# Value products a step later, query products first, the next input transposed in the gate bank, and TensorE's loop from step 80

## The reference

```python
x = x + tanh(g_xattn[0]) * L0_xattn(layernorm(x), ctx, mask)   # 32 query heads, 8 kv heads of 128
x = x + tanh(g_ffn[0])   * L0_ffn(layernorm(x))                # MX fp6 x fp4 weights, silu(gate) * up, then down
x = x + tanh(g_xattn[1]) * L1_xattn(layernorm(x), ctx)
x = x + tanh(g_ffn[1])   * L1_ffn(layernorm(x))                # columns permuted, int4 weights

# L1_xattn: q = h @ Wq.T, k = ctx @ Wk.T, v = ctx @ Wv.T, by heads
q, k = rmsnorm(q, q_norm_w), rmsnorm(k, k_norm_w)              # per head
probs = softmax(q @ k.T / sqrt(128) + mask)
out = (probs @ v) @ Wo.T
```

## Time and profile before

| what | value |
|---|---|
| median of three runs | 1319.82 us |
| profiled execution, its span | 1320.3 us, 1318.5 us |
| TensorE matmul busy | 1302.9 us, 99% of the span |
| VectorE (DVE) busy | 1001.4 us, 76% |
| ScalarE (ACT) busy | 867.4 us, 66% |
| GpSimd (POOL) busy | 621.9 us, 47% |
| chain that ended last: TensorE, GpSimd, VectorE, DMA | 76%, 6%, 5%, 3% |

### The profile page before, as it was taken

How to read it: one execution, slowest core, us unless ns; L and a number is a source line. 1 busy time by engine, 2 the same in 40 slices (tenths; PEclk the granted TensorE clock), 3 DMA queues, 4 the chain that set the end, 5 groups by cost and what they waited for, 6 DMA issues and landing times.

```text
span 1318.5 us, 25473 instructions
## 1 busy us (share of the span) xinstructions
PE 1302.9 (99%) x7477; PEld 1102.0 (84%) x7493; DVE 1001.4 (76%) x2106; ACT 867.4 (66%) x3356; POOL 621.9 (47%) x683
## 2 busy tenths in 40 slices
PE   8999999999999999999999999999999999999999
PEld 7888888888888888877777788888888888888887
DVE  6878787887878788688888858777767677677656
ACT  5767667676767776645566456777767767676551
POOL 2546566565656666446677533532323323332232
DMA  7011110211121121020301013532232222321101
GB/s 297 1 57 55 63 55 20 68 48 68 50 68 50 35 71 33 13 64 20 103 20 48 20 48 89 161 64 77 60 67 69 40 70 57 80 56 32 17 8 56
DMA packets 87340, 78.34 MB, mean 59 GB/s; under 512 B 70880, under 2 KB 75872, under 8 KB 83168
## 3 DMA queue, kind: packets, MB, share of 16 engines
q1 hardware_dynamic: 70272, 71.91, 18.6%
q10 hardware_dynamic: 16672, 4.46, 1.6%
q0 software_dynamic: 320, 1.05, 0.2%
HBM read 57.48 MB, written 3.15 MB: 46 GB/s over the span
## 4 chain that ended last, share of the span: by engine, by line
PE 76%; issue 8%; POOL 6%; DVE 5%; DMA 3%; ACT 1%; POOLq 0%; ACTq 0%; DVEq 0%; SPq 0%
PE bank L1298 54%; PE bank L1362 6%; PE bank L1290 6%; PE bank L1393 6%; PE bank L1324 2%; DMA p_turned<-p_planes 2%; POOL w_lo L551 2%; POOL rstd L580 2%; PE bank L1479 1%; PE bank L1379 1%; POOL fw_y L591 1%; POOL fw_y L589 1%; DVE probs L1138 1%; ACT squares L769 1%; DMA ctx_raw<-in_ctxT 0%
## 5 line engine op out<-in xcount | busy, mean ns | idle before, releaser
L551 POOL TENSOR_TENSOR w_lo<-w_raw,w_hi (+1 forms) x150 | 192.8, 1303 | 164.7 <-ACT w_hi L730 164.7
L769 ACT ACTIVATE squares<-bank 128x128 bf16<-128x128 f32 x512 | 134.4, 278 | 184.7 <-PE bank L1298 184.5
L711 ACT ACTIVATE probs<-probs,negmax 128x128 f32<-128x128 f32 x512 | 198.2, 391 | 7.1 <-DVE negmax L1010 4.5
L576 POOL TENSOR_TENSOR meansq<-sumsq,scalars 128x5 f32<-128x5 f32 x128 | 27.5, 215 | 354.1 <-ACT squares L769 354.1
L580 POOL TENSOR_TENSOR rstd<-meansq,scalars 128x5 f32<-128x5 f32 x128 | 153.2, 1197 | 10.7 <-POOL meansq L576 1.1
L1298 PE MATMUL bank<-w_hi,oT_hi 128*128 (+1 forms) x512 | 150.9, 416 | 0.0
L1298 PE MATMUL bank<-w_hi,xT_hi 128*128 (+1 forms) x512 | 140.3, 395 | 0.0
L1298 PE MATMUL bank<-w_lo,xT_hi 128*128 (+1 forms) x512 | 138.1, 390 | 0.3
L1362 PEld LDWEIGHTS bank<-kT,qT 128*128 128x128 f32 x1024 | 131.7, 191 | 7.7
L1298 PE MATMUL bank<-w_hi,oT_lo 128*128 (+1 forms) x512 | 138.0, 391 | 0.0
L1298 PE MATMUL bank<-w_lo,oT_hi 128*128 (+1 forms) x512 | 137.6, 390 | 0.0
(11 more groups left out here) (129 smaller groups left out, 3073.1 us busy)
## 6 DMA issues: line engine op xcount, KB each, us to landing
w_raw<-in_wq SPq DMA_DIRECT2D x16, 1024.0 KB, 4.8
w_raw<-in_wo SPq DMA_DIRECT2D x16, 1024.0 KB, 9.8
w_raw<-in_wkv SPq DMA_DIRECT2D x16, 512.0 KB, 5.6
fw_raw<-in_ffn_w SPq DMA_DIRECT2D x36, 192.0 KB, 2.3
x_sb<-in_x SPq DMA_DIRECT2D x7, 256.0 KB, 10.7
ctx_raw<-in_ctxT SPq DMA_DIRECT2D x7, 256.0 KB, 9.7
fw_raw<-in_ffn_w SPq DMA_DIRECT2D x7, 256.0 KB, 2.7
out<-x_sb SPq DMA_DIRECT2D x7, 256.0 KB, 2.0
```

The lines of the kernel that those rows point to most:

```text
L551: last = nc.gpsimd.tensor_tensor(lo, raw, hi.bitcast(FP32), ALU.subtract)
L576: nc.gpsimd.tensor_tensor(meansq[:, :], sumsq[:, :], eps_sb[:, :], ALU.add).then_inc(ms_done, 1)
L711: last = nc.scalar.activation(probs[:, h * P:(h + 1) * P], probs[:, h * P:(h + 1) * P], ACT.Exp, bias=negmax[:, h:h + 1], accum_out=rowsum ...
L769: last = nc.scalar.activation(squares[:, h // 2, (b + 1) % 4, h % 2, :], q_bank(n, kind)[:, h * P:(h + 1) * P], ACT.Square, scale=SCALE, a ...
```

## The change

Four edits, of which the last is small:

- **Value products late.** In the PLAIN steps and the steps 76 to 124 (`values_late`) TensorE does the query products first, then the first third of the key/value products, then the value products of unit n-3 (before: of unit n-2, at the end of the step), the rest of the key/value products, scores, output, transposes of k and q. On ACT the squares of q come first, then `oT_hi`, the square of k, `v_hi`; `p_whole` and `pT_hi` go to the end of the step, behind `qT`. On DVE `pT_lo` goes ahead of the planes, and `p_whole` to the end of the step; the int4 work and `wp_lo` (one step later) move ahead of `oT_lo`.
- **Next input in the gate products' bank.** The transposes of the next layer's input use psA instead of psC. They wait for the hidden values of the feed-forward (`gated`) instead of for the accumulation of its output (`d_acc`), and the down products no longer wait for their reader; the gate products do.
- **TensorE's loop from step 80.** Its program has the PLAIN loop from step 80 on (five iterations in place of four); the other engines' loops stay at 88.
- One weight piece moves from step 81 to 82, one from 82 to 83; the normalising of the first batch for the int4 product moves ahead on DVE.

```diff
@@ pieces of the weights
-              32: ((E + 1, 6), (E + 1, 7)), 33: ((E + 1, 8), (E + 1, 9), (E + 2, 0)), 34: ((E + 2, 1), (E + 2, 2)),
-              35: ((E + 2, 3),), 36: ((E + 2, 4), (E + 2, 5)), 37: ((E + 2, 6),), 38: ((E + 2, 7), (E + 2, 8)),
+              32: ((E + 1, 6), (E + 1, 7)), 33: ((E + 1, 8), (E + 1, 9)), 34: ((E + 2, 0), (E + 2, 1)),
+              35: ((E + 2, 2), (E + 2, 3)), 36: ((E + 2, 4), (E + 2, 5)), 37: ((E + 2, 6),), 38: ((E + 2, 7), (E + 2, 8)),
@@ steps
-        def run_steps(eng, step, drain=None):
+        def run_steps(eng, step, drain=None, plain=ZONE1):
...
-            for s in range(ZONE0, ZONE1):
+            for s in range(ZONE0, plain):
...
+        def values_late(n, kind):
+
+            return kind == PLAIN or (isinstance(n, int) and DMA0 < n <= DMA1)
...
         def xT_bank(m):
-            return psC
+            return psA if BATCHES <= m < 2 * BATCHES else psC
@@ ACT
+                    if values_late(n, kind):
+                        q_squares(n, b, kind)
+                        output_upper(n)
                     act.wait_ge(kv_ps, n + 1)
...
                     act.wait_ge(qk_ps, n + 1)
                     nc.scalar.activation(qT[:, :], psSQ[:, :], ACT.Copy).then_inc(qT_sb, 1)
+                if has(n, 2) and by_dma(n, kind):
+
+                    act.wait_ge(pv_ps, n - 2)
+                    act.wait_ge(planes_turned, (n - DMA0 + 1) * 16)
+                    nc.scalar.activation(halves(p_whole[:, :])[:, :, 1], p_turned[:, 0:KT, :].rearrange("p k t -> p (k t)"),
+                                         ACT.Copy).then_inc(upper_placed, 1)
+                    act.wait_ge(upper_placed, n - DMA0 + 2)
+                    act.wait_ge(lower_placed, n - DMA0 + 2)
+                    nc.scalar.activation(pT_hi[:, :], p_whole[:, :], ACT.Copy).then_inc(pt_hid, 1)
@@ DVE
+            def whole_lower(n):
+
+                dve.wait_ge(pt_hid, n - 2)
+                nc.vector.tensor_tensor(pT_lo[:, :], p_whole[:, :], pT_hi[:, :].bitcast(FP32),
+                                        ALU.subtract).then_inc(pt_lod, 1)
+
+            def output_lower(n):
+
+                dve.wait_ge(o_hid, n - 2)
+                nc.vector.tensor_tensor(oT_lo[:, :], psPO[:, :], oT_hi[:, :].bitcast(FP32),
+                                        ALU.subtract).then_inc(o_lod, 1)
...
+                if by_dma(n, kind) or t.last == 0:
+                    scaled_probs(n)
+                if values_late(n, kind):
+                    whole_lower(n)
                 if by_dma(n, kind):
-                    scaled_probs(n)
                     probs_planes(n)
+                for k in gathered(n - 1, kind):
...
+                if kind == ZONE and 0 <= n - INT4_0 < INT4_PARTS and values_late(n, kind):
+                    int4_weights(n - INT4_0)
+                if values_late(n, kind):
+                    output_lower(n)
@@ TensorE
+                        if c == 0 and i >= 2:
+                            pe.wait_ge(xT_lod, BATCHES + i - 1)
...
+                def values(lag=2):
+                    pe.wait_ge(pt_lod, n + 1 - lag)
+                    if lag == 3:
+                        pe.wait_ge(o_lod, n - 3)
+                    slot = (b - lag) % 4
...
+                    if values_late(n, kind):
+                        queries()
+                        wait(pe, kT_sb, n)
+                        keys_values(slice(0, KT))
+                        values(3)
+                        keys_values(slice(KT, 3 * KT)).then_inc(kv_ps, 1)
...
-                    pe.wait_ge(d_acc, t.next + 1)
-                    transposes(qn, psC, ident[:, :]).then_inc(xT_ps, 1)
+                    pe.wait_ge(gated, len(CHUNKS) * min(t.next + 2, BATCHES))
+                    transposes(qn, psA, ident[:, :]).then_inc(xT_ps, 1)
...
-                    if t.next is not None:
-                        pe.wait_ge(xT_lod, BATCHES + t.next + 1)
```

More of the change, by code:

```diff
@@ L730, in split_upper, with q_squares, output_upper @@
                     nc.scalar.activation(hi, raw, ACT.Copy).then_inc(split_hi, 1)
+            def q_squares(n, b, kind):
+                act.wait_ge(q_ps, n + 1)
+                wait(act, rs_done, n)
+                if values_late(n, kind):
+                    act.wait_ge(qk_ps, n)
+                for h in range(REP):
+                    dump = (qn[:, h * P // 2:(h + 1) * P // 2].bitcast(BF16) if values_late(n, kind)
+                            else squares[:, h // 2, (b + 1) % 4, h % 2, :])
+                    last = nc.scalar.activation(dump, q_bank(n, kind)[:, h * P:(h + 1) * P], ACT.Square, scale=SCALE,
+                                                accum_out=sumsq[:, h:h + 1])
+                return last
+            def output_upper(n):
+                act.wait_ge(pv_ps, n - 2)
+                wait(act, y_ps, n - 3)
+                nc.scalar.activation(oT_hi[:, :], psPO[:, :], ACT.Copy).then_inc(o_hid, 1)
             def step(n, b, kind, j, q=None):
@@ L734, in step @@
                 exp_late = calm(n, kind) or (kind == FIRST and b == BATCHES - 1)
[L735 to L739, removed]
+                if has(n, 3) and not values_late(n, kind):
+                    output_upper(n)
                 if calm(n, kind) or (kind == ZONE and n == FFN0):
@@ L764, in step @@
                     hidden_turned(0, t.down)
[L765 to L771, removed]
+                if has(n, 0) and not values_late(n, kind):
+                    q_squares(n, b, kind).then_inc(sq_done, 1)
                 if t.first is not None:
@@ L781, in step @@
                     gate_tanh(2, t.down)
[L782 to L790, removed]
                 if has(n, 2) and not by_dma(n, kind):
@@ L1028, in place_lower, with last_normalised, probs_lower @@
                                       ).then_inc(lower_placed, 1)
-            def probs_lower(n, kind=None):
+            def last_normalised(i):
+                wait(dve, xT_ps, 2 * BATCHES + i if i else 0)
+                normalise(NORM["last", i], i, f_s[:, :])
+            def whole_lower(n):
[6 more added lines that the diff above has]
+                                        ALU.subtract).then_inc(o_lod, 1)
+            def probs_lower(n):
                 dve.wait_ge(pt_hid, n - 1)
-                nc.vector.tensor_tensor(pT_lo[:, :], (p_whole if by_dma(n, kind) else psPO)[:, :], pT_hi[:, :].bitcast(FP32),
+                nc.vector.tensor_tensor(pT_lo[:, :], psPO[:, :], pT_hi[:, :].bitcast(FP32),
                                         ALU.subtract).then_inc(pt_lod, 1)
@@ L1096, in step @@
                     row_inverse(n)
-                if has(n, 2) and not t.active and not by_dma(n, kind):
+                if has(n, 2) and not t.active and not by_dma(n, kind) and t.last != 0:
                     scaled_probs(n)
@@ L1105, in step @@
                         ctx_lower(t.first)
-                if kind == ZONE and 0 <= n - INT4_0 < INT4_PARTS:
+                if kind == ZONE and 0 <= n - INT4_0 < INT4_PARTS and not values_late(n, kind):
                     int4_weights(n - INT4_0)
[L1108 to L1112, removed]
                 if t.first is not None:
@@ L1115, in step @@
                     normalise(t.first, t.first, f_s[:, :])
-                if t.last is not None:
-                    wait(dve, xT_ps, 2 * BATCHES + t.last if t.last else 0)
-                    normalise(NORM["last", t.last], t.last, f_s[:, :])
+                if t.last is not None and t.last:
+                    last_normalised(t.last)
                 if t.norm is not None:
@@ L1149, in step @@
                 if has(n, 2) and qn_first(n, kind, t) and not calm(n, kind):
[L1150 removed]
+                    probs_lower(n)
                 if t.next is not None:
@@ L1524, in _ @@
             first_q(0, slice(2 * KT, 3 * KT)).then_inc(q_ps, 1)
-            run_steps(pe, step)
+            run_steps(pe, step, plain=ZONE1 - BATCHES)
 _SHAPES_OUT = [((BATCHES, P, D), "float32")]
```

69 lines of the change are left out of this document (37 added, 32 removed).

## The result

The changed kernel took 1340.35 us (median of four runs, 1338.17 to 1342.37) against 1319.99 before: a ratio of 1.0156, 95% interval 1.0142 to 1.017. The forecast was no difference, 1320.8, with a range to 1327. It was wrong, by some 20 us. The profiled execution has a span of 1340.6 us.

A forecast was written before the change was run, and what follows sets the result against it. TensorE is busy nearly throughout, so its products plus waits bound the kernel. 1320.3 - 7.7 + 1.9 + 6.75 + 0.06 = 1321.3, less 0.5 to the median: 1320.8 us; no difference 1317.2 to 1322.5, range 1311.5 to 1327.

The forecast's parts named there:

- the branch: TensorE's loop: one added branch costs 0.06 us, so the skill's rule on taken branches breaking instruction fetch moves nothing.
- What goes: TensorE, steps 75 to 124: stalls from late k-transpose landings (7.25) and the f_s wait (0.46) vanish, 7.7 us gained.
- PLAIN's two-piece steps: DVE, 12 PLAIN steps: first plane 0.08 ahead of POOL, one w_lo passes, oT_lo ends at Q+5.5, hidden.
- Steps 77, 78 and 84 to 87: DVE: work ahead of oT_lo meets w_lo; stalls 1.5, 2.0, 1.35 each in 84 and 86, 0.28 each in 85 and 87; 6.75 us.
- Steps 79 to 83: ZONE: 0.03 us between planes and POOL's w_lo left undecided; half the 0.75 stall taken, 1.9 us, bounds 0 and 3.75.
- The floor: TensorE's undisturbed step stays at 9.06 us, since the products are the same; 1.5 us either way over 49 steps.
- The bank: Next input's transposes waiting for the hidden values: 0.29 us to spare in a feed-forward step, so 0.
- The loop from 80: TensorE's loop starting at step 80 adds one branch, 0.06 us.
- POOL gets in first in the PLAIN loop too: Rival, DVE's planes: 12 PLAIN steps pay 0.75 each, five ZONE steps pay in full, 1331.7; range 1322.5 to 1332, chance 0.25.

The follow-up runs named there:

- experiment 1: Changed kernel without the second wait on rs_done that its q_squares brought into every step before 76: 1324.49 us, ratio 1.0044.
- experiment 2: Changed kernel with 24 more waits on ACT, on a semaphore long reached, in steps 80 to 85: 1324.49 us, ratio 1.0042.
- experiment 3: Kernel before with 108 more waits on ACT, on a semaphore long reached, in steps 79 to 87: 1323.24 us, ratio 1.0037.
- experiment 10: Kernel of experiment 6 with TensorE's loop from step 88 again instead of 80: 1314.22 us, ratio 0.9964.
- experiment 4: Kernel before with only TensorE's loop from step 80: 1316.49 us, ratio 0.9979.
- experiment 5: Kernel of experiment 1 with DVE's int4 work and wp_lo moved from ahead of oT_lo to behind the scaling of q: 1320.5 us, ratio 1.0007.
- experiment 9: Kernel of experiment 1 with POOL's weight pieces of steps 77 to 87 also waiting for DVE's pT_lo: 1320.04 us, ratio 1.0005.
- experiment 7: Kernel before with only the next input's transposes moved to the gate products' bank: 1319.27 us, ratio 1.0004.
- experiment 6: Kernel of experiment 1 with late steps' weight pieces later: w_hi on ACT behind v_hi, w_lo on POOL behind rstd: 1313.65 us, ratio 0.9959.
- experiment 8: Kernel of experiment 1 with six more waits on POOL ahead of the first w_lo of each step 76 to 87: 1325.03 us, ratio 1.0046.

## Why the prediction was wrong, by its steps

**The step that failed** is the branch: "The branch here shows 0.06, so by the trace that rule moves nothing." It read TensorE's branch only and asked what one branch more costs. The change also lengthens ACT's program, in every step and inside its loop, and no term of the sum asked whether ACT's loop would still keep its code. Experiments 1 and 2 put 15.9 us on it (1340.35 to 1324.49, medians). The profiled executions of the changed kernel and of experiment 1 lie 18.2 us apart (1342.37 and 1324.15): some 14 in the three steps, and 3.6 in steps 51 and 52, where TensorE waits 1.7 us for `kn` and then runs at the lower clock. That second part is not the change's: a DMA of weights that it does not touch took 7.3 us to land there, 5.2 in experiment 1, and the kernel before waits 0.8 us at the same place. What the other executions lost there was not traced, so the price of ACT's loads is known as 14 to 16 us. The Trainium skill, "Runtime: NRT & Kernel Launch", "Instruction fetch mechanics", says that a taken branch to code that isn't in the engine's window makes it wait for a fetch: the stop of 2.70 us right behind ACT's branch agrees. The second stop, of 2.04 us, comes some instructions later and is not what that sentence speaks of. So the rule that I set aside was the one that spoke against this change. That the place of the loop's body decides is shown both ways (experiments 2 and 3). How much code the engine keeps, and where its limits lie, was not measured.

Without ACT's loads the change costs 1324.49 - 1319.17 = 5.3 us, where the sum had 1.0 (8.65 + 0.06 - 7.7). Term by term:

- *What goes, 7.7:* right. From step 76 on no wait for `kn` or `pT_lo` is left, and experiment 10 shows a late landing without cost. That the code loads make the landings late, of which the prediction saw one case, holds for all seven (experiment 4). One reading was wrong without harm to the sum: the longest wait in the earlier trace rows, 0.8, is the one in step 51, where no transposing DMA runs yet; the other five make 1.8 us and are at most 0.5.
- *PLAIN's two-piece steps, 0:* right. Planes of 1.85 us (1.9 forecast), no wait.
- *Steps 77, 78 and 84 to 87, 6.75:* right. In experiment 1 they are 1.4, 2.0, 1.4, 0.3, 1.4 and 0.3 us above 9.1: 6.7. Experiment 5 shows that the added work ahead of `oT_lo` is what sets them above the others.
- *Steps 79 to 83, half of 3.75 (1.9):* mis-sized. POOL came first in steps 79, 81, 82 and 83, and each lost its whole stall: 0.8, 0.8, 0.8 and 0.9, together 3.3. A gap of 0.03 us that is made by the same durations in every step is no coin to be tossed; the whole stall should have been taken. Experiment 9 shows that the tie decides it. Step 80 lost 0.9 by its late weights, a wait for which the sum had no term.
- *The floor, 0:* mis-sized. A step takes 9.09 to 9.10 in place of 9.06, some 0.04 over 49 steps, 2 us; the bound was 1.5. By the starts in an undisturbed step of experiment 1, the transpose of k in front of those of q and the query products behind them take 0.18 more than before (0.08 and 0.10), the key/value products and the values 0.18 less, and the rest 0.03 more; the reason is not shown.
- *The bank, 0:* right (experiment 7). *The loop from 80, 0.06:* alone it gains 2.7 (experiment 4), of which 1.3 because TensorE's code loads end sooner (the rest is not settled); next to the late values it gains nothing measurable (experiments 6 and 10).

Added up: 6.7 + 3.3 + 0.9 + 2.0 - 7.7 = 5.2, where 5.3 was measured. The rival "POOL gets in first in the PLAIN loop too" gave 1331.7 by a mechanism that did not occur.

## What to carry to other kernels

When a change adds even a wait to an engine's program, count that engine's instructions inside and ahead of each loop, and look in the trace for instruction packets that come back in every iteration; a stop marked "issue" right behind a branch is the sign. When two engines share a resource and their starts are set by the same chain, a few hundredths of a microsecond decide the order every time, so take the order that the durations give and move one of them out of the way. The two steps together made 1340.35 into 1313.65 with all four edits kept: 15.9 us by moving ACT's loop (experiment 1), 10.8 by moving the weight pieces (experiment 6).

## What the runs showed that I had not expected

- ACT's code came in packets of 8 KB (12 packets, 0.10 MB), and two of them stopped the engine for about 2 us each behind a branch; 12 instructions more ahead of the loop took them away, and 15.9 us with them.
- Waits of nearly the same length left TensorE's clock at either level. Behind the wait of 3.67 us in step 96 the granted clock was 0.66 over 5 us, behind that of 3.47 in step 104 it was 1.00; behind the wait of 1.68 us in step 51 it was 0.66, behind that of 1.72 in step 78 1.00, full speed, from 826 to 829 us.
- A transposing DMA landed 0.9 to 1.8 us late when a packet of TensorE's code began 1.1 to 2.7 us after its issue (kernel before, seven of seven).
- Six extra waits on a semaphore long reached did not delay POOL's `w_lo` (experiment 8), since POOL was through with them 7.6 us earlier; a wait for `pT_lo`, which was not yet done, did by 0.2 us.
